# Attention on one Trainium2 core: value products in two parts of two heads, and the shared bank's work moved to the end of a unit

## The reference

```python
x = x + 0.5 * _L0_ffn_ref(_layernorm(x, axis=-1), ...)
x = x + _L0_attn_ref(_layernorm(x, axis=-1), ...)
x = x + 0.5 * _L0_ffn_ref(_layernorm(x, axis=-1), ...)

def _L0_attn_ref(x, Wq, bq, Wk, bk, Wv, bv, Wo, bo, head_mask):   # x is (16, 512, 128), 16 heads of 8
    q = (x @ Wq.T + bq).reshape(b, s, HEADS, HEAD_DIM)
    k = (x @ Wk.T + bk).reshape(b, s, HEADS, HEAD_DIM)
    v = (x @ Wv.T + bv).reshape(b, s, HEADS, HEAD_DIM)
    attn = jnp.einsum('bqhd,bkhd->bhqk', q, k) / np.sqrt(HEAD_DIM).astype(np.float32)
    attn = jax.nn.softmax(attn, axis=-1)
    attn = attn * head_mask[None, :, None, None]
    out = jnp.einsum('bhqk,bkhd->bqhd', attn, v).reshape(b, s, HIDDEN)
    return out @ Wo.T + bo
```

## Time and profile before

| what | value |
|---|---|
| median of 3 runs | 2099.72 us (2094.6 to 2109.0) |
| the profiled execution, own time | 2100.33 us |
| its span, first to last instruction | 2098.1 us |
| mean granted TensorE clock | 0.929 of full |
| PE busy | 1860.1 us (89%) |
| VectorE (DVE) busy | 1496.2 us (71%) |
| ScalarE (ACT) busy | 1232.2 us (59%) |
| GpSimd (POOL) busy | 887.4 us (42%) |

### The profile page before, as it was taken

The page is one execution under the profiler, slowest core; times in us unless marked ns, Lnnn a source line. Parts: engine busy times, 40 slices in busy tenths (PEclk is TensorE's granted clock), DMA queues, the critical chain, the costliest instruction groups (busy, mean ns, idle before and its releaser), DMA issues. The chain is left out here.

```text
span 2098.1 us, 30450 instructions
## 1 busy us (share of the span) xinstructions
PE 1860.1 (89%) x9600; PEld 1108.9 (53%) x9600; DVE 1496.2 (71%) x2379; ACT 1232.2 (59%) x1914; POOL 887.4 (42%) x875
## 2 busy tenths in 40 slices
PE   3999999999937898999999988888859999999999
PEld 2777777777812333333333333333247777777777
DVE  4767777687517878777787777887447768776775
ACT  3566455555513767666676667776635565556654
POOL 2566555655621222222222222221125565556655
PEclk9999999999955989888888889998879999999999
DMA  2000000000032323222223223222010000000000
GB/s 91 21 11 31 27 24 30 10 30 10 16 59 33 47 47 47 47 42 39 41 44 44 41 41 40 53 44 35 12 36 21 31 11 31 20 30 10 30 14 16
DMA packets 43167, 68.57 MB, mean 33 GB/s; under 512 B 9916, under 2 KB 11444, under 8 KB 43060
## 3 DMA queue, kind: packets, MB, share of 16 engines
q1 hardware_dynamic: 38256, 65.15, 15.7%
q0 software_dynamic: 4096, 1.08, 0.3%
q10 hardware_dynamic: 708, 0.98, 0.1%
HBM read 28.36 MB, written 12.58 MB: 20 GB/s over the span
## 5 line engine op out<-in xcount | busy, mean ns | idle before, releaser
L1259 DVE TENSOR_REDUCE attn_neg_max<-attn_p_score 128x2 f32<-128x1024 f32 x512 | 624.8, 1223 | 211.2 <-PE attn_p_score L941 209.1
L572 POOL TENSOR_TENSOR ffn_hid_low<-ffn_hidden,ffn_hid_high 128x512 fp32r<-128x512 f32 x448 | 580.6, 1298 | 454.9 <-ACT ffn_hid_high L512 454.2
L1096 ACT ACTIVATE attn_exps<-attn_p_score 128x1024 f32<-128x1024 f32 x512 | 519.8, 1025 | 286.6 <-PE attn_p_score L927 284.6
L512 ACT ACTIVATE ffn_hid_high<-ffn_hidden 128x512 fp32r<-128x512 f32 x448 | 281.0, 627 | 255.7 <-DVE ffn_hidden L705 254.8
L503 ACT ACTIVATE ffn_silu<-ffn_p_gate 128x512 f32<-128x512 f32 x448 | 264.0, 589 | 207.8 <-PE ffn_p_gate L375 207.5
L698 DVE TENSOR_TENSOR ffn_gated<-ffn_silu,ffn_p_up 128x512 f32<-128x512 f32 x352 | 240.6, 684 | 175.1 <-PE ffn_p_up L375 112.2
L941 PE MATMUL attn_p_score<-k_pack,q_pack 24*128 24x512 f32 x1024 | 283.2, 553 | 57.7 <-ACT attn_exps L1096 33.0
L958 PE MATMUL attn_p_o<-attn_exps,values 128*32 128x512 f32 x2048 | 312.0, 684 | 8.4 <-ACT attn_o_raw L1102 3.3
L927 PE MATMUL attn_p_score<-q_pack,k_pack 26*128 26x512 f32 x1024 | 271.2, 539 | 14.9 <-DMA q_pack<-attn_max_rows 14.6
L927 PEld LDWEIGHTS attn_p_score<-q_pack,k_pack 26*128 26x128 f32 x1024 | 101.4, 198 | 314.7 <-issue 207.5
L705 DVE TENSOR_TENSOR ffn_hidden<-ffn_gated,ffn_p_spread 128x512 f32<-128x512 f32 x352 | 241.2, 685 | 14.9 <-PE ffn_p_spread L416 4.1
(11 more groups left out here) (146 smaller groups left out, 2220.9 us busy)
## 6 DMA issues: line engine op xcount, KB each, us to landing
q_pack<-attn_q_high SPq DMA_DIRECT2D x128, 64.0 KB
k_pack<-attn_k_high SPq DMA_DIRECT2D x128, 64.0 KB
ffn_x_in<-in_x SPq DMA_DIRECT2D x16, 256.0 KB, 2.8
ffn_x_res<-in_x SPq DMA_DIRECT2D x16, 256.0 KB, 2.8
after_ffn<-ffn_x_out SPq DMA_DIRECT2D x16, 256.0 KB, 2.0
attn_x_in<-after_ffn SPq DMA_DIRECT2D x16, 256.0 KB, 4.6
k_pack<-attn_k_low SPq DMA_DIRECT2D x64, 64.0 KB
q_pack<-attn_q_low SPq DMA_DIRECT2D x64, 64.0 KB
```

Source lines behind the costliest of these rows:

```text
L512: nc.scalar.activation(hid_high[s][0:n, :], hidden[s][0:n, :], ACT.Copy).then_inc(high_ready, 1)
L572: nc.gpsimd.tensor_tensor(hid_low[s][0:n, :], hidden[s][0:n, :], hid_high[s][0:n, :].bitcast(F32), ALU.subtract).then_inc(low_ready, 1)
L1096: nc.scalar.activation(exps[n % len(exps)][:], score_bank("exp", b, n)[:], ACT.Exp, scale=inv_sqrt)\
L1259: V.tensor_reduce(neg_max[g % 2][:, j:j + 2, t], score_bank("max", b, n)[:], AX.X, ALU.max, negate=True).then_inc(max_read, 1)
```

## The change

The value products of a unit are called in two parts: heads 0 and 1 of the quad in half 0 of the next unit, heads 2 and 3 in half 1. Each part runs after the scores of its half. The piece of a unit is now called at the end of half 1, after the second part; before, it stood in half 0. On PE each of the 14 pieces is given one unit less than before, so each stands half a unit sooner. The tables of ScalarE and VectorE are moved to match; ScalarE's `copy_max` now stands right behind `copy_o`, in the same half. The lists of GpSimd and of the DMA queue are unchanged.

```diff
-            def times_values(b, u):
+            def times_values(b, u, half):
 
                 g, t = divmod(u, NT)
-                pe.wait_ge(exp_ready, b.count(PAIRS, 2 * (u + 1)))
-                if t == 0:
+                pe.wait_ge(exp_ready, b.count(PAIRS, 2 * u + half + 1))
+                if t == 0 and half == 0:
                     need(pe, o_copied, b.count(NQ, g))
...
-                for h in range(QUAD):
+                for h in (2 * half, 2 * half + 1):
                     last = nc.tensor.matmul(p_o[h * COLS:(h + 1) * COLS, :],
...
-                last.then_inc(pv_done, 1)
+                if half == 1:
+                    last.then_inc(pv_done, 1)
...
                         score_exp(b, u, half)
                         if there(ahead):
                             score_max(ahead, v, half)
-                        if half == 0:
+                        if u > 0:
+                            times_values(b, u - 1, half)
+                        elif not is_first:
+                            times_values(a, UNITS - 1, half)
+                        if half == 1:
                             pieces(b, u, is_first)
-                        elif u > 0:
-                            times_values(b, u - 1)
-                        elif not is_first:
-                            times_values(a, UNITS - 1)
...
-                if u == 1:
+                if u == 0:
                     turn_max(b, 1, uses(b, "m1"))
...
-                if now == (1, 0) and not is_first:
-                    copy_o(a, 3, uses(a, "o1") + 1)
-                if now == (1, 1):
+                if now == (1, 0):
+                    if not is_first:
+                        copy_o(a, 3, uses(a, "o1") + 1)
                     copy_max(b, 1, uses(b, "m1"))
```

More of the change, by code:

```diff
@@ L945, in score_max @@
                 last.then_inc(max_tile, 1)
-            def times_values(b, u):
+            def times_values(b, u, half):
                 g, t = divmod(u, NT)
-                pe.wait_ge(exp_ready, b.count(PAIRS, 2 * (u + 1)))
-                if t == 0:
+                pe.wait_ge(exp_ready, b.count(PAIRS, 2 * u + half + 1))
+                if t == 0 and half == 0:
                     need(pe, o_copied, b.count(NQ, g))
-                if u == 0:
+                if u == 0 and half == 0:
                     first_batch = isinstance(b.j, int) and b.k == 0
@@ L1012, in pieces @@
             def pieces(b, u, is_first):
                 a, c, e = b.step(-1), b.step(1), b.step(2)
-                if u == 1:
+                if u == 0:
                     turn_max(b, 1, uses(b, "m1"))
                 if not is_first:
+                    if u == 1:
+                        turn_o(a, 3, uses(b, "o3"))
                     if u == 2:
-                        turn_o(a, 3, uses(b, "o3"))
+                        turn_norm(uses(b, "norm"))
                     if u == 3:
-                        turn_norm(uses(b, "norm"))
-                    if u == 4:
@@ L1022, in pieces @@
                         project_out(uses(b, "out"))
+                if u == 4:
+                    turn_max(b, 2, uses(b, "m2"))
                 if u == 5:
-                    turn_max(b, 2, uses(b, "m2"))
-                if u == 6:
                     turn_o(b, 0, uses(b, "o0"))
-                if u == 7 and there(c):
+                if u == 6 and there(c):
                     project_v(uses(b, "v"))
-                if u == 8 and there(e):
+                if u == 7 and there(e):
                     turn_x(e, uses(b, "x"))
+                if u == 8:
+                    turn_max(b, 3, uses(b, "m3"))
@@ L1031, in pieces @@
                 if u == 9:
-                    turn_max(b, 3, uses(b, "m3"))
-                if u == 10:
                     turn_o(b, 1, uses(b, "o1"))
+                if u == 10 and there(e):
+                    project_qk(e, w.wq, uses(b, "q"))
                 if u == 11 and there(e):
-                    project_qk(e, w.wq, uses(b, "q"))
-                if u == 12 and there(e):
                     project_qk(e, w.wk, uses(b, "k"))
-                if u == 13 and there(c):
+                if u == 12 and there(c):
@@ L1058, in _ @@
             every_batch(pe, batch)
-            times_values(end, UNITS - 1)
+            times_values(end, UNITS - 1, 0)
+            times_values(end, UNITS - 1, 1)
             turn_o(end, NQ - 1, last_uses)
@@ L1116, in pieces @@
                 now = (u, half)
-                if now == (1, 0) and not is_first:
-                    copy_o(a, 3, uses(a, "o1") + 1)
-                if now == (1, 1):
+                if now == (1, 0):
+                    if not is_first:
+                        copy_o(a, 3, uses(a, "o1") + 1)
                     copy_max(b, 1, uses(b, "m1"))
-                if now == (3, 1) and not is_first:
+                if now == (3, 0) and not is_first:
                     copy_ot(uses(b, "norm"))
```

40 lines of the change are left out of this document (19 added, 21 removed).

## The result

The changed kernel takes 2303.1 us (median of 4 runs, 2301.09 to 2305.5) against 2101.6 us of the kernel before: a ratio of 1.096, 95% interval 1.092 to 1.100. The ratios in this document compare only executions within about 1.5% of the kernel's fastest, so they can differ from the ratio of the medians that stand beside them.

The account below looks back on a forecast made before the run. At the low clock PE itself was taken to bound the attention: units 82.7, pieces 14.7, copy waits 7.4, together 104.8 us a batch. The main part came to 1655 against 871.5 us, giving 2888 us; range 2540 to 2925.

Parts of the forecast that it names:

- The price of a part: Value products on PE: a part of two heads takes as long as four heads, 1.00 us at full clock.
- The ring: Attention unit at full clock, without pieces: 1.62 + 0.43 + 1.00 = 3.05 us, as before the change.
- half a unit at the low level: PE in the attention at low clock: scores to values 0.72 plus values to scores 1.86, 2.58 us.
- The pieces uncovered: PE at the end of half 1: pieces no longer hidden behind the exponential, 8.3 us a batch at full clock.
- The wait for the copy: Value products in half 0 of units 1, 5, 9, 13 wait for copy_o: 6.6 us a batch at full clock.
- The sum at full clock: Attention's main part wholly at full clock: 63.7 us for a full batch, 1007 us in all.
- The clock: PE in the attention: the stage stays at 1.2 GHz from start to end, 104.8 us a batch; given 0.64.
- the rows of 977.5 to 991.0: Old trace of the attention: PE busy 13.39 of 13.50 us while the grant stays 0.50; evidence for the low clock.
- The fall after the wait: PE idle stretches at 63 waits for the copy: at full clock the level would also fall again; no size given.
- the first rival: Attention at full clock, if a busy PE is enough to bring it back: +135, 2236 us; chance 0.09.
- a mixture nearer to full level: Attention partly at each clock level, nearer to full: 2300 to 2540 us; chance 0.06.
- full level nearly throughout: Attention at full clock nearly all the time: 2200 to 2300 us; chance 0.09.

Follow-up runs that it names:

- e3: The changed kernel with all four heads in both parts, so every value product is made twice; 2275.8 us, ratio 1.085.
- e8: The changed kernel with one head in each part from batch 1 on, half of the value products left out; 2287.8 us, ratio 1.097.
- e2: The changed kernel with copy_o one place earlier on ScalarE, ahead of the exponential of units 1, 5, 9 and 13, half 0; 2138.4 us, ratio 1.020.
- e9: The kernel before with value products in two parts of two heads, pieces and tables as before; 2308.4 us, ratio 1.109.
- e4: The kernel before with the value products of heads 2 and 3 of every quad left out from batch 1 on; 2101.4 us, ratio 1.000.
- e1: The changed kernel with value products in one part of four heads again, in half 1, pieces still at the unit's end; 2182.0 us, ratio 1.041.
- e5: The changed kernel with copy_o one place earlier and each part cut as all four heads by 256 of 512 queries; 2124.1 us, ratio 1.021.
- e6: The kernel before with two parts of four heads by 256 queries, copy_o one place earlier, pieces in half 0; 2135.8 us, ratio 1.028.
- e10: The kernel before with four unread transposes added in half 0 of units 15 and 0; 2082.7 us, ratio 0.997.

## Why the prediction was wrong

**The price of a part** was right: 0.98 us measured at full clock, 1.00 forecast. e3 and e8 show it from one head to four.

**The ring** was right: 3.02 us without a piece, 3.05 forecast. So was half a unit at the low level: 2.58 us from value products to value products (652.21 to 654.79 below), 2.58 forecast.

**The pieces uncovered**: 8.3 us a batch forecast. e2 runs at full level with nearly no other wait; 908.7 us for 16 batches, of which the last two and the first have fewer pieces, is 57.4 us for a full batch by the starts of its exponentials, 57.1 forecast (16 x 3.05 + 8.3). Right, though two small errors cancel in part: by the ring of 3.02 the pieces come to some 9.1 us, of which the moved copies are about 0.3. What I did not say is that the parts alone would uncover the pieces too (e9).

**The wait for the copy**: 1.66 us on the ring forecast, about 1.4 measured; idle time 1.69 against the 1.83 of the earlier trace rows. Right in kind, a little too dear.

**The sum at full clock**, 1007 us for the main part, is what the runs give, added up from two of them: e2's 908.7 and 89 for the waits are 998.

**The clock** is the step that failed: "the stage stays at 1.2 GHz from start to end". The first low stretch ended 8.5 us into the main part, and the mean there is 0.91; this took 585 us off the forecast of 2888. It rested on the rows of 977.5 to 991.0, where a busy PE did not bring the clock back, and on the reading that it took many products in a short time. The changed kernel showed at once that this reading is wrong. PE's timeline at its first units:

```profile
652.21 1.92 PE L958 MATMUL attn_p_o<-attn_exps,values 128*32 128x512 f32 x4
654.06 0.79 PE L927 MATMUL attn_p_score<-q_pack,k_pack 26*128 26x512 f32 x2
...
654.79 1.92 PE L958 MATMUL attn_p_o<-attn_exps,values 128*32 128x512 f32 x4
656.64 0.79 PE L927 MATMUL attn_p_score<-q_pack,k_pack 26*128 26x512 f32 x2
...
657.37 1.30 PE L958 MATMUL attn_p_o<-attn_exps,values 128*32 128x512 f32 x4
658.60 0.50 PE L927 MATMUL attn_p_score<-q_pack,k_pack 26*128 26x512 f32 x2
```

Two heads at a time, no piece among them (the last one, a short transpose of maxima, stands at 651.15), and the clock rises at 657.9. In the kernel before, value matmuls of four heads ran in one half of two; here they run in every half, 1.92 of each 2.58 us. It is their running time that the change doubles, while the products stay the same. e4 (half of the products, nothing changed) and e8 against e3 (a quarter of the products, 12 us apart) show that the number of products is not what the clock goes by.

That it goes by the time that matmuls other than the scores run (value products and pieces) fits all the traces. Where parts of all 512 queries stand in both halves (the changed kernel, e2, e3, e8, e9), the stage's first low stretch ended 7 to 9 us into the main part, and no later one was longer than 6.8 us but for one of 10.2 in e3. In the other eight traces the first ended 25 to 55 us into it, and the longest later one lasted 13.7 to 30.7 us. The first low stretch of e1, with one part, and a later one of e8, with one head in a part:

```profile
648.10:702.60 54.50, 47.29 (x194) 15.37 (x192) 29.75 (x38) 23.69 (x29) 9.95 (x15) 0.50 0.06 8
```

```profile
1169.50:1176.30 6.80, 6.44 (x17) 1.84 (x18) 1.35 (x2) 1.55 (x4) 2.43 (x3) 0.50 0.02 5
```

The nearest to a test is e5 against e2: the same products with the copy and the pieces in the same places, but value matmuls that run little more than half as long, and low stretches of up to 27.3 us where e2 has none behind its first. No run changed that time and left the rest, since e5's units are shorter too, so this stays the reading that fits and is not shown by itself.

The Trainium skill's rule, cited in the prediction against itself ("TensorE: Matmul & The Clock Gate", "What's actually happening": activity releases the throttle), named the right side. The rows still don't agree with it word for word if activity is the profile's busy time: 13.39 of 13.50 us stayed low in the kernel before, 7.81 of 8.50 came back here.

**The fall after the wait** was foreseen, but only as a reason for the low level, and left out of the first rival's 2236 us. e2 shows it: with the wait go all falls, and 78 us beside the direct 89. That rival with this term, 2236 + 78 = 2314, is within 11 us of the result; the 78 are known only since e2. The result fell into the case of a mixture nearer to full level, to which I had given 0.06, but only 3 us from its edge at 2300; the case below it, full level nearly throughout, had 0.09.

**The change's own parts.** The direction was right and the mechanism at full clock too. The size failed with the clock alone.

## What to carry to other kernels

Work that is split to balance two halves must be split along the direction in which it takes time: heads that lie side by side in the array's columns cost the same one by one or four at once, so halving them doubles their price, while halving the queries made a part cheaper (0.57 us in place of 0.98). That alone brought no gain on the kernel before. When work moves to an earlier place, look on the other engine at what still stands ahead of what it waits for: here one copy behind one exponential cost 167 of 204 us, and moving four calls on ScalarE took that away. Where the level of TensorE's clock decides a forecast, give both levels real weight unless a run shows which kind of work holds it.

## What the hardware showed that I had not expected

The clock came back within 8.5 us on two-head value matmuls and score matmuls with one short transpose, with half of the columns unused, though in the kernel before it had stayed low for 13.5 us with PE busy 99% of the time, and in e5 for 27.3 us with PE busy throughout. It fell in 43 of the 63 units with one idle stretch of 1.7 us and was mostly back 3.4 us later (1251.8 to 1255.2), and it did not fall once in 905 us of e2, where PE is busy 888. A gain in clock or in PE's time was often given back: with cheaper parts (e5, e6) the clock was lower than in e2, and the better clock of e10 came with 20 us more of DMA waits.
